# Attention scores from four 32-row groups instead of one stacked 128-row product

## What is computed

```
q = layernorm(x) @ W_q.T ; k = ctx @ W_k.T ; v = ctx @ W_v.T          (16 heads of 32)
scores = q k^T / sqrt(32) ; e = exp(clip(scores, -50, 50)) ; attn = e / sum(e)
x = x + (attn @ v) @ W_o.T
y = layernorm(x) ; int8 rows of y times int8 columns of rhs, scaled back ; out = x + y'
```

## Time and profile before

| | |
|---|---|
| median of 3 runs | 1717.78 us (1716.49 to 1719.31) |
| the profiled execution, its own time | 1718.7 us |
| its span in the profile | 1716.7 us |
| TensorE busy | 1677.0 us, 98% |
| VectorE busy | 1489.9 us, 87% |
| ScalarE busy | 1314.5 us, 77% |
| 12 segments of batches 0 to 2 | from about 137 us to 1330 us |

### The profile page before, as it was taken

The page is one execution under the profiler, slowest core; times in us unless marked ns, Lnnn a source line. Parts: engine busy times, 40 slices in busy tenths (PEclk is TensorE's granted clock), DMA queues, the critical chain, the costliest instruction groups (busy, mean ns, idle before and its releaser), DMA issues.

```text
span 1716.7 us, 29869 instructions
## 1 busy us (share of the span) xinstructions
PE 1677.0 (98%) x10418; PEld 1013.5 (59%) x10448; DVE 1489.9 (87%) x1705; ACT 1314.5 (77%) x1730; POOL 133.8 (8%) x75
## 2 busy tenths in 40 slices
PE   8999999999999999999999999999999899999997
PEld 7996655655565665665666565666656344444445
DVE  5657888888898989899898999989899789999996
ACT  5557888888887778878787787787877678787883
POOL 0000000000001111010110101111010010001001
PEclk9999999999999999999999999999999999999999
DMA  7787556566676665756756676665756878988952
GB/s 255 225 232 191 142 144 151 150 168 167 150 174 147 160 179 149 212 129 174 180 136 175 158 186 161 159 176 135 208 135 163 207 169 203 223 175 202 218 146 80
DMA packets 235636, 295.90 MB, mean 172 GB/s; under 512 B 28249, under 2 KB 142425, under 8 KB 234969
## 3 DMA queue, kind: packets, MB, share of 16 engines
q1 hardware_dynamic: 232264, 288.69, 66.2%
q10 hardware_dynamic: 3216, 5.24, 1.1%
HBM read 201.59 MB, written 92.00 MB: 171 GB/s over the span
## 4 chain that ended last, share of the span: by engine, by line
PE 81%; DVE 6%; DMA 5%; ACT 5%; issue 2%; SPq 1%; POOL 0%; ACTq 0%; DVEq 0%
PE tile L965 24%; PE wsum L1002 24%; PE scores L987 21%; ACT probs L1251 4%; DVE acc L1554 4%; PE scores L1151 3%; PE scores L965 2%; PE tile L1034 1%; PE tile L1151 1%; DMA o_parts<-sums 1%; DMA row_lo<-o_parts 1%; PE tile L1114 1%; PE tile L1091 1%; PE scores L626 1%; DMA den_c<-denoms 1%
## 5 line engine op out<-in xcount | busy, mean ns | idle before, releaser
L1251 ACT ACTIVATE probs<-scores 128x1024 f32<-128x1024 f32 x939 | 914.7, 1026 | 208.0 <-PE scores L987 168.9
L1554 DVE TENSOR_TENSOR acc<-acc,probs 128x2048 f32<-128x2048 f32 x439 | 1003.4, 2286 | 40.3 <-ACT probs L1251 25.8
L1002 PE MATMUL wsum<-probs,v_sb 128*32 128x512 f32 x4096 | 493.4, 599 | 0.0
L987 PE MATMUL scores<-q_stack,k_stack 128*128 128x512 f32 x1536 | 444.5, 409 | 2.5 <-ACT probs L1251 1.7
L987 PEld LDWEIGHTS scores<-q_stack,k_stack 128*128 128x128 f32 x1536 | 265.1, 188 | 212.8 <-ACT probs L1251 121.2
L1002 PEld LDWEIGHTS wsum<-probs,v_sb 128*32 128x32 f32 x4096 | 107.2, 109 | 243.6 <-issue 229.8
L1656 POOL TENSOR_TENSOR rstd<-var_eps,minus_half 128x1 f32<-128x1 f32 x48 | 106.0, 2208 | 1187.3 <-DVE var_eps L1448 1187.3
L1554 DVE TENSOR_TENSOR acc<-probs 128x2048 f32<-128x2048 f32 x32 | 73.4, 2293 | 56.5 <-PE tile L1034 51.2
L1151 PE MATMUL scores<-q_stack,k_stack 128*128 128x512 f32 x342 | 110.4, 424 | 10.5 <-ACT probs L1251 10.5
L965 PE MATMUL tile<-ctx_hi,wk_hi 128*128 128x256 f32 x412 | 116.5, 283 | 0.0
L965 PE MATMUL tile<-ctx_hi,wk_lo 128*128 128x256 f32 x412 | 116.1, 282 | 0.0
(11 more groups left out here) (247 smaller groups left out, 1990.2 us busy)
## 6 DMA issues: line engine op xcount, KB each, us to landing
k_stack<-k_parts SPq DMA_DIRECT2D x312, 256.0 KB, 7.6
q_stack<-q_parts SPq DMA_DIRECT2D x124, 256.0 KB, 7.3
v_sb<-v_parts SPq DMA_DIRECT2D x80, 256.0 KB, 7.4
v_parts<-v_stage SPq DMA_DIRECT2D x64, 256.0 KB, 5.0
raw<-ctxT SPq DMA_DIRECT2D x27, 512.0 KB, 6.6
k_parts<-stage_hi SPq DMA_DIRECT2D x96, 128.0 KB, 4.5
k_parts<-stage_lo SPq DMA_DIRECT2D x96, 128.0 KB, 2.4
x_in<-x SPq DMA_DIRECT2D x33, 256.0 KB, 4.8
```

The source lines that it names most:

```text
L987: last = nc.tensor.matmul(scores[:, h, :], k_stack[:, kt // 4, h, (kt % 4) * P:(kt % 4 + 1) * P], q_stack[:, qb, h, :], start=True, stop=True)
L1002: last = nc.tensor.matmul(wsum[DH * h:DH * h + DH, :], v_sb[:, kt, DH * h:DH * h + DH], probs[:, n % RING, h, :], start=(kt == 0), stop=(k ...
L1251: nc.scalar.activation(probs[:, slot % RING, 2 * pair:2 * pair + 2, :], score_banks(seg, slot, pair), ACT.Exp, scale=1.0 / math.sqrt(DH)). ...
L1554: nc.vector.tensor_tensor(acc[:, :, :], other, probs[:, slot % RING, :, :], ALU.add).then_inc(sems["add_done"], 1)
```

## The change

In the attention of batches 0, 1 and 2 the scores are no longer made from stacked copies. `k_stack` and `q_stack` hold, for these, head h in rows 32h to 32h+31, with the hi and the lo part side by side in the free dimension. A step's scores are 12 products over 32 rows: three rounds (hi by hi, lo by hi, hi by lo) of four heads, where the heads of a round stand in different rows of the array and write different banks, and the three rounds of a head accumulate in its bank. The product lo by lo is left out. The order is by rounds: all four heads of a round before the next round. `load_k` and `load_q` issue two DMAs instead of four for these batches. Batch 3 keeps the stacked form.

On ScalarE the piece of the odd step is copied out after the exponentials of the odd step, where before it came ahead of them. On VectorE the work on the odd step's piece comes after the odd step's `add`, where before it came ahead of it. Both are as before in a visit that ends with a `split` in its odd step (`ends`).

```diff
--- before.py
+++ after.py
@@ -277,9 +277,9 @@
     **{f"x_loaded{n}": (lambda g, n=n: 16 * (g.has("load_x", n) + g.has("load_x", n + 2) + (g.s == 0))) for n in range(2)},
     "raw_loaded0": lambda g: 16 * g.has("load_raw", 2), "raw_loaded1": lambda g: 16 * (g.has("load_raw", 1) + (g.s == 0)),
     "orows_loaded": (0, 0, 32), "xr_loaded": (0, 0, 32),
-    **{f"k_loaded{n}": (lambda g: 64 * g.b * (1 + g.final)) for n in range(4)},
+    **{f"k_loaded{n}": (lambda g: 128 if g.final else 32 * g.b) for n in range(4)},
     **{f"v_loaded{n}": (lambda g: 16 * g.b * (1 + g.final)) for n in range(4)},
-    "q_loaded0": (0, 64, 0), "q_loaded1": (0, 64, 0),
+    **{f"q_loaded{n}": (lambda g: 64 if g.final else 32 * g.b) for n in range(2)},
 
     **{f"{part}_stored{n}": (lambda seg, n=n: 0 if not seg.a else 16 * STAGED // 4 if not seg.b else 16 * STAGED // 2 if n < 2 else 0)
        for part in ("hi", "lo") for n in range(4)},
@@ -706,9 +706,17 @@
                 if n >= FULL + 3:
                     add_rows(pool, nc.gpsimd.tensor_tensor, n - 3)
 
+        def stacked(j):
+
+            return j >= (B - 1) * G
+
         def load_k(eng, j, quarter):
 
             src = k_parts[j, :, :, quarter * 4 * P:(quarter + 1) * 4 * P]
+            if not stacked(j):
+                for part in range(2):
+                    eng.dma_start(k_stack[:, quarter, part, :].bitcast(F32), src[part]).then_inc(sems[f"k_loaded{quarter}"], 16)
+                return
             for part in range(2):
                 for twice in range(2):
                     at = 64 * twice + 32 * part
@@ -718,6 +726,10 @@
         def load_q(eng, j, qb, half=None):
 
             src, at = q_parts[j, :, :, qb * QB:(qb + 1) * QB], qb if half is None else half
+            if not stacked(j):
+                for part in range(2):
+                    eng.dma_start(q_stack[:, at, part, :].bitcast(F32), src[part]).then_inc(sems[f"q_loaded{at}"], 16)
+                return
             for r in range(4):
                 eng.dma_start(q_stack[DH * r:DH * r + DH, at, :, :].bitcast(F32),
                              src[r // 2].rearrange("(h d) t -> d h t", d=DH)).then_inc(sems[f"q_loaded{at}"], 16)
@@ -978,15 +990,19 @@
 
                     qb, kt = divmod(n, KT)
                     if kt == 0:
-                        ct.wait(pe, f"q_loaded{qb}", 64)
+                        ct.wait(pe, f"q_loaded{qb}", 32)
                     if qb == 0 and kt % 4 == 0:
-                        ct.wait(pe, f"k_loaded{kt // 4}", 64)
-                    for pair in range(2):
-                        ct.wait(pe, "exp_done", 2 * n + pair - 1)
-                        for h in (2 * pair, 2 * pair + 1):
-                            last = nc.tensor.matmul(scores[:, h, :], k_stack[:, kt // 4, h, (kt % 4) * P:(kt % 4 + 1) * P],
-                                                    q_stack[:, qb, h, :], start=True, stop=True)
-                        last.then_inc(sems["scores_full"], 1)
+                        ct.wait(pe, f"k_loaded{kt // 4}", 32)
+                    keys = slice((kt % 4) * P, (kt % 4 + 1) * P)
+                    for term, (k_part, q_part) in enumerate(((0, 0), (1, 0), (0, 1))):
+                        for h in range(G):
+                            if not term and h % 2 == 0:
+                                ct.wait(pe, "exp_done", 2 * n + h // 2 - 1)
+                            rows = slice(DH * h, DH * h + DH)
+                            last = nc.tensor.matmul(scores[:, h, :], k_stack[rows, kt // 4, k_part, keys], q_stack[rows, qb, q_part, :],
+                                                    start=(term == 0), stop=(term == 2))
+                            if term == 2 and h % 2:
+                                last.then_inc(sems["scores_full"], 1)
 
                 def sums_of(n):
 
@@ -1321,9 +1337,9 @@
                 for even in range(0, STEPS, 2):
                     if seg.b:
                         exponentials(even)
-                        for p in seg.pieces(even) + seg.pieces(even + 1):
+                        ends = ("split", 1 + even // KT) in seg.at(even + 1) and even % KT == KT - 2
+                        for p in seg.pieces(even) + (seg.pieces(even + 1) if ends else []):
                             evacuate(p)
-                        ends = ("split", 1 + even // KT) in seg.at(even + 1) and even % KT == KT - 2
                         if ends:
                             for p in seg.at(even + 1):
                                 work(p)
@@ -1334,6 +1350,8 @@
                         if n is not None:
                             copy_turned(act, n, dsum)
                         exponentials(even + 1)
+                        for p in [] if ends else seg.pieces(even + 1):
+                            evacuate(p)
                         for slot in (even, even + 1)[:1 if ends else 2]:
                             for p in seg.at(slot):
                                 work(p)
@@ -1611,16 +1629,17 @@
                     if seg.b:
                         add(even)
                         ends = ("split", 1 + even // KT) in seg.at(even + 1) and even % KT == KT - 2
-                        for soon in (True, False):
-                            for slot in (even, even + 1):
-                                for p in seg.at(slot):
-                                    if (p[0] in SOON or ends and p[0] in ("bound", "split")) == soon:
-                                        row_work(p)
-                                    if p[0] == "F" and not soon:
-                                        ct.wait(dve, "y_scaled", p[1] + 1)
-                                        nc.vector.tensor_tensor(normed[:, :], normed[:, :], xr[:, :], ALU.add).then_inc(sems["y_added"], 1)
-                            if soon:
-                                add(even + 1)
+                        for slot, soon in ((even, True), (even + 1, True), (even, False), (even + 1, False)):
+                            if soon and slot % 2 and not ends:
+                                add(slot)
+                            for p in seg.at(slot):
+                                if (p[0] in SOON or ends and p[0] in ("bound", "split")) == soon:
+                                    row_work(p)
+                                if p[0] == "F" and not soon:
+                                    ct.wait(dve, "y_scaled", p[1] + 1)
+                                    nc.vector.tensor_tensor(normed[:, :], normed[:, :], xr[:, :], ALU.add).then_inc(sems["y_added"], 1)
+                            if soon and slot % 2 and ends:
+                                add(slot)
                     else:
                         for slot in (even, even + 1):
                             for p in seg.at(slot):
```

## The result

The changed kernel takes 1774.01 us (median of 4 runs, 1770.98 to 1776.15) against 1717.79 us: 1.0326 times as long, 95% interval 1.0308 to 1.0344, 56 us more. Forecast were 1794 us and a range of 1738 to 1835.

The account below looks back on a forecast made before the run. The prediction took TensorE to bound the kernel before. It added 46 us (wait for heads 2 and 3), 12 (ScalarE's other work) and 20 (row of step 5), less 2 (DMA): 76 us more, 1794 us, range 1738 to 1835.

Parts of the forecast that it names:

- The scores and changes of tiling: TensorE per visit: scores stream 0.54 us less, two new tiling changes cost 0.20 each; 3.77 + piece time, 0.14 less.
- partly overlapping rounds: Rival for the score products: four-head rounds overlap only in part, 0.30 us each; 71 us more, 1865 us; chance 0.08.
- serial weight loads: Rival for the score products: a round's four weight loads go one after another; 242 us more, 2036 us; chance 0.03.
- The wait for heads 2 and 3: Between a step's exponentials and the next: a 1.02 us gap makes steps at least 2.96 us; 46 us loss over all visits.
- ScalarE's other work: Copies and splits must fit the gaps between exponentials; where they overflow, 1 us a segment is lost, 12 us in all.
- The row of step 5: Batches 1 and 2: the add ahead of piece O delays `quant`, `whole` and piece V; 2.5 us a segment, 20 us.
- The clock: Whole kernel: granted clock at its upper level, 2.4 GHz, in every slice, so no gain or loss from it.
- DMA: Key and query loads: half as many transfers, 2 us gained at the borders of batches.
- TensorE remains the bound: Rival for back halves: exponentials plus gap stay under TensorE's 2.71 us; 27 us less, 1691 us, faster; chance 0.08.
- the signs that the prediction named: Profile after: ScalarE gap about 1.0 us, short-piece visits 5.9, `whole` waiting 2 to 3; wrong if gap under 0.8, back half 2.7.

Follow-up runs that it names:

- tiles64: The kernel before with scores in two strips of 64 rows, same columns streamed, so four tiling changes a visit for two: 1783.05 us, ratio 1.0372.
- lagged: The changed kernel with the products of heads 2 and 3 ordered one round behind those of heads 0 and 1: 1772.90 us, ratio 1.0305.
- scores_only: The kernel before with the new scores and loads, but the old orders on ScalarE and VectorE: 1751.41 us, ratio 1.0201.
- spot_no: As spot_n, with VectorE's old order also in steps 4 and 5 of the segments of batches 1 and 2: 1761.05 us, ratio 1.0251.
- spot_n: The changed kernel with VectorE's old order back in steps 28 and 29 of each batch's last segment, ahead of piece N: 1768.16 us, ratio 1.0293.
- exp_short: The changed kernel with exponentials of only 448 of 512 queries in batches 0 to 2: 1745.83 us.

## Why the prediction was right, and where not

The direction and its main mechanism were right: two dearer changes of tiling, and a wait that puts ScalarE's exponentials onto the path. The sum was 76 us and the loss 56; term by term:

**The scores and changes of tiling.** Rounds overlap wholly, but one begins every 0.235 us, not 0.22: it is the interval of the 128-row products (0.23), not half of the 0.43 of the value products, and far from the 1.30 products that one rival had for a round. A change costs 0.19 to 0.20, as taken (tiles64). TensorE alone thus needs 3.77 + 0.09 = 3.86 + p in a visit, for 3.91 + p. K and a third of V has 6.22 us by it, and 6.22 to 6.23 stands in the table where nothing waits. The rivals of partly overlapping rounds and of serial weight loads fall with it.

**The wait for heads 2 and 3, the step that was mis-sized.** The prediction has a gap of 1.02 us between a step's exponentials and the next, with 0.44 in it "for two rounds until the third begins", and so a back half in which "the exponentials of the odd step decide with 2.96". That did not hold. Here is ScalarE's timeline of the changed kernel in batch 0, the even step of one visit at 295.49 and the odd one before it:

```profile
292.02 1.94 ACT L1267 ACTIVATE probs<-scores 128x1024 f32<-128x1024 f32 x2
...
295.49 1.94 ACT L1267 ACTIVATE probs<-scores 128x1024 f32<-128x1024 f32 x2 [0.81 <-PE scores L1002]
298.26 1.94 ACT L1267 ACTIVATE probs<-scores 128x1024 f32<-128x1024 f32 x2 [0.84 <-PE scores L1002]
```

The gap is 0.84 and not 1.02. The starts of the twelve products of the last step say why: two at 297.24, two at 297.48, two at 297.58, four at 297.82 and two at 298.05 us. The first two are heads 0 and 1. The exponentials that heads 2 and 3 wait for end at 297.43, and the weight load that carries this wait is recorded at 297.48, so the two products of that time are the first of heads 2 and 3; their records are 0.49 us long, with the load in them, where those behind have 0.39 to 0.41. The two at 297.58 are already the second round of heads 0 and 1, whose third starts at 297.82. Heads 0 and 1 are thus a round ahead of heads 2 and 3 and stay so, and only one round, 0.24, lies between the load and their third, where the prediction had two, 0.44: 0.05 to the load, 0.10 for it, 0.24 for the round and 0.44 to the exponentials are 0.83. A step's exponentials and their gap are 2.78 us, and against TensorE's back half, 2.75 us by the starts of its products, they hardly decide. A short visit is the front half, from its scores to the end of their exponentials (1.00 + 1.94 + 0.05 = 2.99 us), and a back half of TensorE alone (2.75): 5.74 us, as measured, for 5.92 forecast. Shortened exponentials take 0.21 off once, 5.53, also as measured; and a shorter gap (lagged) doesn't show. A long visit is held up by 0.2 us at its first scores, if the odd scores before it started all four heads at once: 6.22 + 0.23 = 6.45. That costs more than the 0.11 forecast (0.18), the short visits less (0.39 to 0.48 for 0.58 to 0.64). Over all visits 46 us were forecast; scores_only measured 34.5. It is in part luck that these are so near: for K and a third of V the forecast 6.38 has a back half that is 0.21 too long and leaves out the hold-up of 0.23. Of the 34.5 us, 3.5 are in the very first visit of batch 0, for which the sum has no term: in scores_only TensorE is granted 0.50 from 141 to 145 us and 0.65 from there to 149, in the kernel before 1.00.

**ScalarE's other work**, 12 us: 4.5 with the new scores, 0 without.

**The row of step 5**, 20 us: 7 by spot_no, 5 by the visits. The stop of the bank at piece V was seen rightly, 0.66 us for 0.6. What failed is the length of GpSimd's power, taken from the earlier trace rows: 2.58 us there, and its wait at `whole`, 2.1 us of the 2.5 in a segment. In the changed kernel it is a fifth of that:

```profile
665.52 0.15 DVE L1466 TENSOR_SCALAR var_eps<-mean_var 128x1 f32<-128x1 f32 x1
666.34 0.55 DVE L1487 TENSOR_SCALAR x_in<-x_in,mean_var,rstd 128x512 f32<-128x512 f32 x1 [0.66 <-POOL rstd L1675]
...
665.76 0.55 POOL L1675 TENSOR_TENSOR rstd<-var_eps,minus_half 128x1 f32<-128x1 f32 x1 [4.13 <-DVE var_eps L1466]
...
669.00 0.63 ACT L1289 ACTIVATE q<-normed 128x512 bf16<-128x512 f32 x1 [0.45 <-DVE normed L1505]
```

In the kernel before, VectorE's add ran at the same time (637.10 to 639.39), and the power ended 0.41 us behind it; now VectorE stands still and waits for the power. ScalarE waited 0.45 us for `quant`, not 2.5.

**Not seen at all**: the stop at piece N, 6 us by spot_n, and those of steps 0, 1, 22 and 23, some 4 us by the visits. I had gone through the pieces for who waits for VectorE's odd one at a single place, the O piece. The rule that a moved add stands ahead of everything behind it held at three more. VectorE's order thus costs 16 to 18 us, near the 20 forecast, but only 5 to 7 of them are at the place that the 20 were for: that is luck.

**The clock** was put at nothing, as the page prints a 9 for every slice. It does so after the change too. A slice is 44 us long and hides the stretches at N: there the products and scores took 1.23 + 0.47 = 1.7 us more than at the upper level, by estimate 5 us for the three. The first visit of batch 0 is another such place (above).

**DMA**: no gain for the 2 us counted.

Of the rivals, "TensorE remains the bound" would by these measured terms have been 192 x 0.05 = 10 us faster; the waits for the exponentials take that back several times over: a visit with one K takes 5.74 us where TensorE alone needs 3.86 + 1.43 = 5.29, and exp_short takes 28 us off. (That ScalarE waits longer for scores, 275.9 us for 168.9, doesn't show it; that is the wait of the other engine.)

Of the signs that the prediction named, some came and some didn't: ScalarE's gap is 0.84 for 1.0, over the 0.8 that was to show it wrong; visits with one K took 5.74 us for 5.9; `whole` waited 0.45 us for 2 to 3; and the back half, 2.75, is nearly the 2.7 that was to show it wrong. Where the exponentials decide is the front half of a short visit.

## What to carry to other kernels

Price a product cut into row strips by its changes of tiling and by what its completion order does to the engine that reads the result, not by the columns streamed alone: 0.45 us saved in the streams of a visit were all but gone by two changes of 0.2 us. When a wait moves up, do the sum for each half of the loop and ask which engine arrives last there; a gap on the path in one half can be idle time in the other. When an instruction of 2 us is moved ahead of another on an in-order engine, list all who wait for the second, not the first one found.

## What was not expected of the hardware

- Products in different row strips don't hold to the program's order beyond their own strip. In lagged, the second round of heads 0 and 1 is written ahead of the first of heads 2 and 3. In program order the starts would come in groups of two, four, four and two; in a step without a wait they come in three groups of four (268.35 to 268.36, 268.68 to 268.70 and 268.91 to 268.93 us), and the step's scores take no more time than by rounds. The load of heads 2 and 3 is recorded at 268.36, those of the second round of heads 0 and 1 only at 268.45. In the changed kernel heads 0 and 1 run a round ahead of heads 2 and 3 while these wait (297.24 to 298.05 us, above).
- GpSimd's power of 128 values takes 0.55 us when VectorE is idle (665.76 us, above), and also beside VectorE's short work on a piece (0.55 at 698.43 us). Beside VectorE's add it takes 2.58 and ends 0.41 behind the add.
- Of the 3.0 us that a stop at N adds to its visit, over half is the clock: products of 1.87 us took 3.10, with 0.57 granted.
